# Lookup hash split by token pair: the first two sequences alone, the others beside the first layers

## What is computed

```
# 1. embedding: six n-gram lookups, n = 3..8, in tables of 25000 rows of 128
hash = sum_j float32(byte[t+j]) * 256**j      # float32 sum in a fixed order
idx  = int32(hash % 25000)
mean = sum_n table_n[idx] / n * sigmoid(gate_n) / 6    # nothing for t > 512 - n
h0   = concat(byte_emb[byte], mean) @ W_enc.T + b_enc
# 2. three layers: layernorm, retention with 4 heads and a decay mask,
#    group norm, gate, output projection; layernorm, 128-512-128 FFN with gelu
# 3. router: x + h0, norm, argmax of 8 logits; each token through its expert
```

## Time and profile before

| | us |
|---|---|
| median of 3 runs (2426.34 to 2426.5) | 2426.39 |
| profiled execution | 2424.55 |
| its span | 2422.7 |
| TensorE busy | 2223.8 (92%) |
| VectorE busy | 1869.4 (77%) |
| GpSimd busy | 1762.4 (73%) |
| ScalarE busy | 1550.3 (64%) |

### The profile page before, as it was taken

How to read it: one execution, slowest core, us unless ns; L and a number is a source line. 1 busy time by engine, 2 the same in 40 slices (tenths; PEclk the granted TensorE clock), 3 DMA queues, 4 the chain that set the end, 5 groups by cost and what they waited for, 6 DMA issues and landing times.

```text
span 2422.7 us, 52427 instructions
## 1 busy us (share of the span) xinstructions
PE 2223.8 (92%) x18306; PEld 1940.9 (80%) x18306; DVE 1869.4 (77%) x5586; ACT 1550.3 (64%) x4986; POOL 1762.4 (73%) x1758
## 2 busy tenths in 40 slices
PE   0389999999999999999999999999999999996984
PEld 0268888888888888888888888888888888886874
DVE  6457888878787888888888888787888887867543
ACT  0156776776767777677677776767777677763442
POOL 4786777777777777777777777777777774334777
PEclk9989999999999999999999999999999999998997
DMA  2813131312122222213131313122221111002875
GB/s 98 311 40 101 25 112 29 111 29 96 44 72 67 72 69 71 72 29 111 27 112 27 110 30 113 28 72 66 72 69 36 34 28 36 1 30 79 254 229 158
DMA packets 110527, 192.17 MB, mean 79 GB/s; under 512 B 24388, under 2 KB 44998, under 8 KB 110160
## 3 DMA queue, kind: packets, MB, share of 16 engines
q1 hardware_dynamic: 66640, 97.96, 11.6%
q0 software_dynamic: 33280, 67.45, 9.9%
q10 hardware_dynamic: 10368, 23.67, 3.3%
HBM read 100.30 MB, written 89.73 MB: 78 GB/s over the span
## 4 chain that ended last, share of the span: by engine, by line
PE 74%; POOL 11%; DVE 5%; issue 5%; ACT 3%; DMA 2%; ACTq 1%; POOLq 0%; SPq 0%; DVEq 0%
PE psum L1211 64%; PE psum L1231 7%; POOL grams L621 4%; POOL gr L656 3%; PE psum L1282 3%; POOL out L683 2%; DVE hid L1058 2%; ACT qm L736 1%; DMA out<-h,e_id 1%; ACT qkT L734 1%; ACT xn L747 1%; POOL rstd L632 0%; DVE ms L1063 0%; DMA out<-side_n,e_id 0%; ACT hid L790 0%
## 5 line engine op out<-in xcount | busy, mean ns | idle before, releaser
L621 POOL DMA_INDIRECT grams<-gram_table,idx_all x768 | 780.4, 1016 | 193.6 <-issue 184.9
L1211 PE MATMUL psum<-xT,lw 128*128 128x256 f32 x1920 | 479.1, 383 | 0.2 <-ACT xT L722 0.2
L656 POOL TENSOR_TENSOR gr<-ms,con 128x8 f32<-128x8 f32 x192 | 325.9, 1697 | 154.7 <-DVE ms L1063 151.4
L1211 PE MATMUL psum<-lw,hid 128*128 128x129 f32 x3072 | 392.7, 277 | 1.9 <-ACT hid L766 1.9
L1211 PEld LDWEIGHTS psum<-lw,hid 128*128 128x128 f32 x3072 | 369.8, 192 | 15.0 <-issue 10.3
L1211 PEld LDWEIGHTS psum<-xT,lw 128*128 128x128 f32 x1920 | 339.1, 191 | 32.0 <-ACT xT L722 0.3
L632 POOL TENSOR_TENSOR rstd<-ss,con 128x2 f32<-128x2 f32 x320 | 232.1, 728 | 173.2 <-ACT squares L710 170.4
L766 ACT ACTIVATE hid<-psum,par 128x256 f32<-128x256 f32 x768 | 307.0, 482 | 10.8 <-PE psum L1211 7.9
L722 ACT ACTIVATE xT<-psum,par 128x256 f32<-128x256 f32 x384 | 214.8, 564 | 122.2 <-PE psum L1231 122.0
L1211 PE MATMUL psum<-lw,xT 128*128 128x256 f32 (+1 forms) x1536 | 287.6, 330 | 0.7 <-ACT xT L722 0.7
L1058 DVE TENSOR_TENSOR hid<-psum,con 128x512 f32<-128x512 f32 x384 | 249.0, 683 | 31.7 <-PE psum L1211 27.4
(11 more groups left out here) (200 smaller groups left out, 4689.1 us busy)
## 6 DMA issues: line engine op xcount, KB each, us to landing
routed_rows<-pad SPq DMA_DIRECT2D x265, 264.0 KB, 4.3
grams<-expert_w ACTq DMA_DIRECT2D x45, 321.0 KB
grams<-gram_table,idx_all POOLq DMA_INDIRECT x768
grams<-routed_rows SPq DMA_DIRECT2D x80, 132.0 KB
qm<-expert_w ACTq DMA_DIRECT2D x27, 321.0 KB
xb<-x SPq DMA_DIRECT2D x32, 256.0 KB, 3.5
lw<-layer_w SPq DMA_DIRECT2D x1, 2503.5 KB, 12.2
routed_rows<-row,slot POOLq DMA_INDIRECT x128, 2.4
```

Source lines behind the costliest of these rows:

```text
L621: pool.indirect_dma_start(grams[s][:, g, c, :], None, gram_table, bass.IndirectOffsetOnAxis(ap=idx_all[:, g, at:at + 1], axis=0))\
L656: pool.tensor_tensor(gr[s][:, c], ms[s][:, c], const("half")[:, 0:n], ALU.pow).then_inc(y_r[s], 1)
L1211: return pe.matmul(dst, lhsT, rhs, start=start, stop=stop)
```

## The change

What the diff does:

- The hash runs twice with its own buffers: `hashes[0]` for the first pair (8 of 128 columns) and `hashes[1]` for the other fifteen (120 columns). Tokens are put on partitions first: TensorE transposes eight shifted windows of the bytes, ScalarE copies them to `win` (8 x 128 columns), and every later step works on columns that are chunks. The six transposes and two index copies at the end go, and one linked copy writes `idx_all`.
- `hash_front(b)` (not shown) holds the steps of L841 to L873 on the buffers `b`, with the bytes read from `win`, in 11 pieces; `hash_middle` and `hash_back` hold those of L876 to L896.
- The first hash runs at once. Then GpSimd waits for its indices, and starts on its main program. The second hash, and the centring of the weights of layers 1 and 2, become a fifth sequence, `setup`, in the order of VectorE and GpSimd, with planner times of its own. TensorE waits for the weights of layers 1 and 2 in the first pair.
- The constants are loaded in three parts, the identity first.
- Pair 1's gathers are timed from 30 by 2.6, where it was from 0 by 4.2, and the first waits for the second hash.
- SP's pads wait for the sums of both halves of the second sequence of pair 0.
- `LAGS`, `EARLY`, `CLOSING` and all entries of `AT` have new values. Starts in `EARLY` move from -15.83, 3.58, 12.53, 32.61 to -28.98, -2.51, 18.9, 32.82; most others move by less than 3, some by tens.

```diff
-LAGS = ((0.13, 11.99), (28.45, 40.29))
-EARLY = ((-15.83, 3.58), (12.53, 32.61))
-CLOSING = ((2.51, 3.01), (1.38, 3.83))
+LAGS = ((0.09, 11.97), (28.45, 40.29))
+EARLY = ((-28.98, -2.51), (18.9, 32.82))
+CLOSING = ((2.87, 3.04), (0.35, 0.57))
...
@@ -285,14 +285,23 @@
             return v if len(shape) == 1 else v.rearrange("p (a n) -> p a n", a=shape[0])
 
         GP = NG * P
-        hv = lent(hid[0], 0, [NG, P])
-        quot = lent(hid[0], GP, [NG, P])
-        lane = lent(hid[0], 2 * GP, [4, P])
-        limb = [lent(hid[1], n * GP, [NG, P]) for n in range(2)]
-        xf = lent(hid[1], 2 * GP, [P + 8])
-        mod_i = [lent(grams[1], n * GP, [NG, P], I32) for n in range(3)]
-        quot_i = lent(grams[1], 3 * GP, [NG, P], I32)
-        limb_i = lent(qk[0], 0, [NG, P], I32)
+        PAIR = 2 * CH
+        REST = rows - PAIR
+        win = sb("win", [P, 8, rows])
+        xf = lent(hid[0], 0, [P + 8])
+
+        def hash_buffers(cols, make):
+            n = cols.stop - cols.start
+            f = [make(k, [NG, n]) for k in range(5)]
+            return dict(cols=cols, n=n, hv=f[0], quot=f[1], limb=f[2:4], quot_i=f[4].bitcast(I32),
+                        mod_i=[f[2].bitcast(I32), f[3].bitcast(I32), f[0].bitcast(I32)], lane=make(5, [4, n]))
+        pair_hash = lent(hid[0], P + 8, [5 * NG + 4, PAIR])
+        rest_hash = [lent(hid[1], 0, [NG, REST]), lent(hid[1], NG * REST, [NG, REST]), sb("rest_limb", [P, NG, REST])]
+        spare_hash = lent(qm[1], 0, [2 * NG + 4, REST])
+        hashes = [
+            hash_buffers(slice(0, PAIR), lambda k, shape: pair_hash[:, k * NG:k * NG + shape[0], :]),
+            hash_buffers(slice(PAIR, rows), lambda k, shape: (rest_hash[k][:, :, :] if k < 3
+                         else spare_hash[:, (k - 3) * NG:(k - 3) * NG + shape[0], :]))]
...
-        def main_program(embed, attend, feed, route, *others):
+        def spaced(part, start, step):
+
+            for n, _ in enumerate(part):
+                yield start + step * n
+
+        def main_program(embed, attend, feed, route, *others, setup=None):
 
             streams = [(s, h, LAGS[s][h]) for s in range(2) for h in range(2)]
             by_progress(*[one_by_one(lag + FIRST, *sequences(s, h, attend, feed)) for s, h, lag in streams],
                         *[one_by_one(EARLY[s][h], *beside(s, h, embed, route)) for s, h, _ in streams],
-                        *[one_by_one(EARLY[s][h], *other(s, h)) for s, h, _ in streams for other in others])
+                        *[one_by_one(EARLY[s][h], *other(s, h)) for s, h, _ in streams for other in others],
+                        *([one_by_one(LAGS[0][0], (setup(), 0))] if setup else []))
...
                          x[0:batches, :].rearrange("b (q t) -> (b q) t", t=P)[1:rows, 0:7]).then_inc(s_x, 16)
-            sp.dma_start(con[:, :], consts).then_inc(s_con, 16)
+            first, last = CONST["eye"].start, CONST["eye"].stop
+            sp.dma_start(con[:, first:last], consts[:, first:last]).then_inc(s_x, 16)
+            for part in (slice(0, first), slice(last, CONST_COLS)):
+                sp.dma_start(con[:, part], consts[:, part]).then_inc(s_con, 16)
             sp.dma_start(par[:, :], params).then_inc(s_par, 16)
             sp.dma_start(lw[:, :, :], layer_w.rearrange("l p n -> p l n")).then_inc(s_lw, 16)
             for s in range(2):
                 sp.dma_start(xb[s][:, :], x[s:s + 1, :].partition_broadcast(P)).then_inc(x_in[s], 16)
-            sp.wait_ge(s_hash_f, 5)
+            sp.wait_ge(s_hash_f, FIRST_SETUP)
+            for h in range(2):
+                sp.wait_ge(acc_step[1][h], NG)
             for block in range(4):
                 pad_block(block, 0)
             sp.dma_start(padded(E * region), pad[:, :, :]).then_inc(e_pad[0], 16)
...
+            done = [2]
+
+            def mod_sum(b, ready):
+
+                def times(k):
+                    return mult_i[:, k:k + 1].unsqueeze(2).to_broadcast([P, NG, b["n"]])
+
+                def after(ins):
+
+                    done[0] += 1
+                    ins.then_inc(s_p, 1)
+                    pool.wait_ge(s_p, done[0])
+                mod_i = b["mod_i"]
+                yield
+                pool.wait_ge(s_hash_f, ready)
+                pool.tensor_tensor(mod_i[0], mod_i[0], times(0), ALU.mult)
+                yield
+                after(pool.tensor_tensor(mod_i[1], mod_i[1], times(1), ALU.mult))
+                yield
+                after(pool.tensor_tensor(mod_i[0], mod_i[0], mod_i[1], ALU.add))
+                yield
+                pool.tensor_tensor(mod_i[0], mod_i[0], mod_i[2], ALU.add).then_inc(s_hash_i, 1)
+
+            def mod_rest(b, ready):
+
+                def times(k):
+                    return mult_i[:, k:k + 1].unsqueeze(2).to_broadcast([P, NG, b["n"]])
+                yield
+                pool.wait_ge(s_hash_f, ready)
+                done[0] += 1
+                pool.tensor_tensor(b["quot_i"], b["quot_i"], times(2), ALU.mult).then_inc(s_p, 1)
+                yield
+                pool.wait_ge(s_p, done[0])
+                pool.tensor_tensor(b["mod_i"][0], b["mod_i"][0], b["quot_i"], ALU.add).then_inc(s_hash_i, 1)
+            for part in (mod_sum(hashes[0], PAIR_MOD), mod_rest(hashes[0], PAIR_QUOT)):
+                for _ in part:
+                    pass
+            pool.wait_ge(s_hash_f, PAIR_IDX)
+
+            def setup():
+                yield from spaced(mod_sum(hashes[1], REST_MOD), 31.5, 1.5)
+                yield from spaced(mod_rest(hashes[1], REST_QUOT), 39, 1)
...
 
             def gathered(it, s, h):
                 for n in range(2 * NG):
-                    yield (1.25 * n - 15, 4.2 * n, LATER_GATHERS[n])[min(it, 2)]
+                    yield (1.25 * n - 15, 30 + 2.6 * n, LATER_GATHERS[n])[min(it, 2)]
+                    if n == 0 and it == 1:
+                        pool.wait_ge(s_hash_f, REST_IDX)
                     if n == 0 and it:
                         pool.wait_ge(acc_step[s][h], it * NG)
...
         def _(act):
+            act.wait_ge(s_hash_T, 1)
+            for part in (slice(0, PAIR), slice(PAIR, rows)):
+                for n in range(2):
+                    last = act.activation(win[:, 4 * n:4 * n + 4, part],
+                                          bank(1, 2 + n).rearrange("p (w c) -> p w c", w=4)[:, :, part], ACT.Copy)
+                last.then_inc(s_gate_t, 1)
             act.wait_ge(s_par, 16)
 
             act.activation(gate[:, :], param("gates"), ACT.Tanh, scale=0.5).then_inc(s_gate_t, 1)
...
+            def hash_middle(b, sums):
+                yield
+                dve.wait_ge(s_hash_i, sums)
+                link(dve.tensor_copy(b["quot"], b["mod_i"][0]))
+                dve.tensor_scalar(b["quot_i"], b["quot"], 1.0 / HASHES, None, ALU.mult).then_inc(s_hash_f, 1)
+
+            def hash_back(b, sums):
+
+                hv, quot, n = b["hv"], b["quot"], b["n"]
+                yield
+                dve.wait_ge(s_hash_i, sums)
+                link(dve.tensor_copy(hv, b["mod_i"][0]))
+                link(dve.tensor_scalar(quot, hv, 0.0, float(HASHES), ALU.is_lt, ALU.mult))
+                link(dve.tensor_tensor(hv, hv, quot, ALU.add))
+                yield
+                link(dve.tensor_scalar(quot, hv, float(HASHES), -float(HASHES), ALU.is_ge, ALU.mult))
+                link(dve.tensor_tensor(hv, hv, quot, ALU.add))
+                yield
+                dve.wait_ge(s_con, 32)
+
+                link(dve.tensor_tensor(hv, hv, const("gram_row").unsqueeze(2).to_broadcast([P, NG, n]), ALU.add))
+                ends = hv.rearrange("p g (s c) -> p g s c", c=CH)[:, :, :, CH - 1]
+                link(dve.tensor_tensor(ends, ends, const("beyond").unsqueeze(2).to_broadcast([P, NG, n // CH]), ALU.max))
+                dve.tensor_copy(idx_all[:, :, b["cols"]], hv).then_inc(s_hash_f, 1)
+
+            def at_once(*parts):
+                for part in parts:
+                    for _ in part:
+                        pass
+            at_once(hash_front(hashes[0]), hash_middle(hashes[0], 1), hash_back(hashes[0], 2))
...
+            def centred_layer(l):
+
+                yield from centre(l)
+                dve.sem_inc(s_hash_f, 1)
+
+            def setup():
+                yield from spaced(hash_front(hashes[1]), 4, 3)
+                yield from spaced(hash_middle(hashes[1], 3), 38, 1)
+                yield from spaced(hash_back(hashes[1], 4), 40, 1)
+                yield from spaced(centred_layer(1), 46, 4)
+                yield from spaced(centred_layer(2), 60, 4)
 
...
 
-            pe.wait_ge(s_con, 16)
-            pe.wait_ge(s_hash_f, 3)
-            for g in range(NG):
-                last = pe.transpose(psum[:, g // 4, (g % 4) * P:(g % 4) * P + P], hv[:, g, :], eye)
+            pe.wait_ge(s_hash_f, BYTES_CAST)
+            for w in range(8):
+                last = pe.transpose(bank(1, 2 + w // 4)[:, (w % 4) * P:(w % 4) * P + P], xf[:, w:w + P], eye)
```

(6 more changed lines are left out.)

178 lines of the change are left out of this document (75 added, 103 removed), and 64 rows, old and new, of the table AT.

## The result

The kernel after takes 2421.77 us (median of 14 runs, 2419.12 to 2422.75), beside 2426.39 of the kernel before on the same chips (14 runs): a ratio of 0.9981 [0.9974, 0.9988], a gain of 4.6 us where 11 were forecast. Its profiled execution took 2422.42 us with a span of 2420.6. The three executions of e12 to e14, the kernel before's own among them, took 4 to 6% longer than all others and are compared only with one another.

The account below looks back on a forecast made before the run. TensorE was taken to bound the steady part, GpSimd the start. Of 23 us earlier gathers about half is given back, 11 kept, other terms 0: 2424.55 - 11 = 2413.55, as a median 2415.4; range 2402 to 2426.

Parts of the forecast that it names:

- Part 4: Second hash beside the first layers: 9.6 us of GpSimd products in the queue and 9 us of idle, bounds 3 and 20.
- Part 1: Hash of pair 0 alone: first gather moves from 40.82 to about 17.6, 23.2 us earlier.
- Part 2: VectorE's setup after the pair's hash: 13.9 us, ending at about 31, hidden behind the first twelve gathers.
- Part 3: Pair 0's 48 gathers without pair 1's between, 1.25 us each, end at 81.3; first layer moves from 94.83 to about 61.
- A rule weighed: VectorE's two-port steps in the second hash lock GpSimd out: up to 8 us more queue, time near 2423; not adopted.
- Part 5: First gather to marker (power gr, stream (1,0), layer 1): 169.4 us, marker at 187, 12 earlier; 11 us gain taken.
- Part 6: Pads behind the first sums, about 87 to 137: hidden, late landings bounded 0 to 4 us, taken as 0.
- Part 7: New instruction order in the steady part and at the end: taken as 0, own bounds -6 and +6 us.
- A: Start: GpSimd's order is not what TensorE waits for, the whole 23 us shift arrives: 2403; chance 0.16.
- C: Start: VectorE and GpSimd hold each other on second hash and ports, idle 18, late landings add 2: 2424; chance 0.14.
- B: Steady part: new order also closes gaps, 0.5 us a pair or more beyond the 11: near 2406; chance 0.14.
- D: Later 15 pairs: new order makes TensorE wait in the mask-scores-values handover, 1.3 us a pair: 2435, slower; chance 0.10.

Follow-up runs that it names:

- e12 to e14: Repeat profiles without edits: the kernel before twice more, the kernel after once; executions took 2531.33, 2580.16 and 2556.9 us.
- e5: Kernel after without GpSimd's six 720-element products and sums of the second hash, only their signals raised: 2418.45 us, 0.9966 of before.
- e11: e9 with the second hash's front products behind VectorE's sum of stream (1,1), quotient and back part behind the first gr: 2420.84 us, 0.9979 of before.
- e4: Kernel after with 24 of pair 1's 48 gathers left out: 2405.61 us, 0.9917 of before.
- e1: Kernel after with LAGS, EARLY, CLOSING and AT of the kernel before, split hash kept: 2424.32 us, 0.9994 of before.
- e3: Kernel after with SP's pads no longer waiting for the first sums: 2423.61 us, 0.9991 of before.
- e9: Kernel after with one table entry, "act v", 8.04 in place of 8.03: 2418.85 us, 0.9967 of before.
- e10: e9 with the CLOSING of the kernel before: 2418.54 us, 0.9967 of before.

## Why the prediction was off

The step that failed is Part 4: the idle time that the second hash makes GpSimd wait, and what it waits for. The direction held, and so did the outline: the hash comes 23 us earlier and part of that is given back in the start. The size did not, 4.6 for 11. Part 4 has the products in the queue that sets the end of this stretch, with 2.2 us of idle in front of the first gr, for VectorE's front steps, and 9 up to the marker. The trace has no wait for front steps; GpSimd waits 7.5 us ahead of the first gr (3.34 for the moments behind the sum of (1,1), 1.69 for the quotient, 2.52 for the squares) and 14.0 up to the marker. The chain that ends last there is VectorE's, behind the landing of the last gather, and the sum of (1,1) that heads it has no place in Part 4's chain. Its 9 also leave out most of the 2.3 us between 90 and 92.3 of its own timeline. Step by step:

- **Part 1** held, pieces too (eight transposes 1.97 for 2.0): first gather 17.86 for 17.6. A 48-element step of VectorE took 0.19 to 0.21, one of GpSimd 0.27 (0.22 with its gap, and 0.25, were taken).
- **Part 2** held: the first sum at 34.59, for its gather and not for the setup.
- **Part 3** nearly: first layer 60.07 for 61, but the 48th gather ends at 83.4 and not at 81.3. The 1.25 taken was below the prediction's own rows: 0.99 busy and 0.3 of issue are 1.29, and the earlier trace rows has 99.3 + 27.4 us for 100, 1.27. Here the 48 take 48.0 + 13.9, 1.29 each, which is 1.9 of the 2.1 us.
- **Part 4 failed.** First gr 102.47 for 96.5, and pair 1's first gather 105.73 for 101.6. VectorE's steps were taken at their usual durations, and their chain was stretched: four steps of the sum from 85.00 took 5.6 us where they need 1.9 (0.35 + 1.53 in e5), because GpSimd's products ran beside them. The term of 9.6 us of products was misplaced too: e5, without them, wins 3.9 and not 9.6. The rest of the 6 us, some 2, is Part 3's late last gather: e5's first gr stands at 98.59.
- **A rule weighed.** The Trainium skill (SBUF — State Buffer, Who interferes with whom) was applied to one direction only, VectorE locking GpSimd out. The same section states the other too: a VectorE instruction with two SBUF inputs contends with a GpSimd instruction that reads SBUF, and the order of issue decides which of them blocks. The trace agrees in both directions. VectorE's steps of two SBUF inputs take 1.86 and 1.80 us beside the products and 0.48 behind them. GpSimd's L642 takes 2.03 us where VectorE's L1120, with two such inputs, began 0.3 before it, and 1.70 in e11. The first cost 3.9 us (e5), the second 0.3 to 0.4 each time, so the 8 us that the prediction weighed did not come; that 2423 is near the measured time is chance.
- **Part 5** held: from the first gr to the marker 90.49 us, 90.5 were forecast (96.5 to 187), so the marker is late by what the first gr is. That the digit agrees is luck. Pair 1's first gather came 3.3 us behind the first gr and not 5.1, and the stretch behind it took 87.2 and not 85.4. In the sum from 17.6 the waits are 5 us more (14.0 for 9) and the queue under 1 (161.1 for 160.4). Its 5.2 us of waits in before leave out the 1.90 ahead of the marker. e4 shows that the queue binds there. e1 shows that the term goes with the new AT: with the old one the stretch takes 98.2 us.
- **Part 6** was taken as 0 between 0 and 4 lost; late pads gain about 2 (e3). With them the last gather of pair 0 ends 0.9 us earlier, the sum behind it begins 1.3 earlier and is stretched by 1.1 less. How pads slow the gathers and front steps was not traced.
- **Part 7** was taken as 0 and is a sum of two: 4.2 us lost in pair 1 (gr 13 to 14), 1.9 won from gr 14 to 191 (1902.0 us for 1903.9; all kernels with the new AT take 1901.8 to 1903.0, those with the old one 1903.5 to 1904.0). The loss is the tie that e9 undoes, though its exact size lies within the scatter of gr 7 to 13. No row of before could show it, but the tables of the diff could.
- **Last stage:** 232.6 us in before's profile, 237.0 in after's. It stays open how much of these 4.4 us the kernel makes: before's profiled execution was 1.84 under its median and after's 0.65 above, so 2.5 us of them may be no more than the two executions. e10 excludes the closing times as the cause.

The account, in us of lead: 12.3 were forecast at the marker, of which 11 were taken for the end. The profile has 6.35 at the marker, short by the 6.0 that the first gr is late; 2.4 are won up to gr 13, 4.2 lost at the tie, 1.9 won up to gr 191: 6.55 there. The last stage takes 4.4, and 2.5 come back between the two profiled executions and the medians: 4.6.

Of the rivals A falls by e4. C was the nearest: it named two engines that hold each other on the second hash and its ports, with idle of 18 us where 14.0 came, and 2421.77 lies nearer its 2424 than the forecast's 2415.4. Its late landings under the pads did not come (e3). B's closing of gaps is there at a quarter of its price (0.13 us a pair). D is not: from gr 14 to 191 the later pairs win 1.9 us together.

## What to carry to other kernels

- When work is moved beside other work, price not only its own queue time but what it does to the steps it runs beside. 9.7 us of products cost nothing on their own queue where they stood and 3.9 through the sum they slowed; moved behind it, they held up the gathers that need them (e11).
- A lead is worth what the next bound queue leaves of it. Find the queue that binds after the moved stretch and count its work from the new start, and the waits beside it by name: the work came out within 1 us of 160, the waits 5 short of 14.
- Where an order comes from sums of floats, look for ties: one entry changed by 0.01 added some 3 us to a gain of 4.6.

## What the hardware showed

- VectorE's three-operand step (128x256, f32) takes 0.48 us alone and 1.80 to 1.86 beside GpSimd's 720-element sums, ending 0.3 us behind each; its scaled copy of the same size, one SBUF tensor and a factor from SBUF, 1.31 for 0.35. Each of these short steps paid up to one whole GpSimd operation.
- GpSimd pays less: its products and sums take 1.39, 1.38, 1.70 and 1.76 beside that sum of VectorE. Only where VectorE's product of two SBUF tensors (L1120) has begun just before do they take longer: 2.03 for 1.70 in the kernel after, 2.14 for 1.70 in e11.
- Small steps cost far more than their share: on GpSimd 48 elements take 0.27 us and 720 take 1.38, on VectorE 0.19 and 0.53.
